# Summing the first layer's results inside the attention block, one group at a time

## The chip, the core and the metric

The kernel runs on one core of one Trainium2 chip. The metric is the device time of one launch in microseconds. The core has TensorE (PE in the profile; its weight loads are PEld), VectorE (DVE), ScalarE (ACT), GpSimd (POOL) and SyncE (SP), which here only issues transfers. Each engine runs its own instruction list in order, and the lists meet at semaphores.

## What is computed

Two layers over x, 32 sequences of 128 steps with 128 channels. In each layer a conditioning part feeds a mixture of experts, and the result is added to x.

```python
x = x + _L0_ffn_ref(_L0_cond_ref(cond_1024, x, ...), ...)       # layer 0: recurrence, then experts
x = x + _L1_ffn_ref(_L1_cond_ref(cond_1024, x, ...), ...)       # layer 1: attention, then experts

# layer 0: h = scan over 128 steps (gates z, r);  moe of 8 experts, top 2, plus 2 shared experts
w = jnp.sum(topk_probs[:, :, None] * onehot, axis=1)
return (shared + jnp.einsum('te,etd->td', w, y)).reshape(B, L, D)

# layer 1, attention
A = softmax(Q2 K2^T / sqrt(D)) - alpha * softmax(A1);  hidden = A @ V
# layer 1, experts: gates = top 2 of softmax(hidden @ wg), a capacity of C rows an expert
buf = zeros((E * C + 1, D)).at[pos].set(xk);  ...;  combined = sum(gates * ybuf[pos])
res = hidden + combined;  layer norm of res
```

## The kernel before

The program is three blocks one behind the other. In each block every engine has a list of its own, and between two blocks all engines meet at a barrier.

**Scan block** (`phase_scan`). The recurrence, layer 0's shared experts and its routed tiles. A tile's 256 result rows go to the DRAM tensor `moe_out` by two indirect transfers of 128 rows that GpSimd issues (`send`, L738 to L746); each row carries its own number, worked out once in `numbers` (L1272). `moe_out` has 2 x 4096 rows of 128 floats: half q holds each token's q-th expert. A row's number is sequence x 128 + step. At the end of the block the two halves are summed and turned, in eight groups of four sequences: SP loads group g of both halves into `yg[g % 3]` (L695), VectorE adds them (`add`, L1354), TensorE transposes four 128 x 128 pieces (`mix`, L916), and VectorE adds what the scan left in `xT` and writes `x1T` (`finish`, L1360). `x1T` is layer 1's input, channels on partitions. SP starts these loads when all results have landed (`y_sent`).

**Attention block** (`phase_attention`). Constants first (`constants`, `constants2`), then a software pipeline over the same eight groups, written out by hand in each engine's list. For group g: ScalarE makes the high part of `x1T` (`high`, L1662), VectorE the low part (`low`, L1722), TensorE queries and keys (`keys`, six matmuls of 512 columns, L351 to L353), values (`values`, 20 matmuls of 136 columns, L1566 to L1572), `scores` (L1588), the transposed weights (`turn_a`, L1579), router logits and hidden states (`attend`, L1598 and L1603), `x1T` turned to rows (`turn_x`, L1610) and the counts of tokens for each expert (`count`, L1619). VectorE picks the experts (`shifted`, `choices`, `gates`) and works out the slots (`places`, L1783 to L1795, which raises `pos_ready`). With `pos_ready` and the hidden states GpSimd issues 8 indirect transfers for the group, each sending 128 rows to their slots (`dispatch`, L327 to L335). Groups 0 to 6 are dispatched in this block, group 7 at the start of the next.

TensorE's order in iteration i is `keys(i+1)`, `values(i+1)`, `turn_a(i)`, `scores(i+1)`, `attend(i)`, `turn_x(i+1)`, `count(i)`. `turn_a` and `turn_x` write the one PSUM bank `bt`. ScalarE's `high(g)` waits for `values(g-1)`, since the tile `xg_hi` is one buffer.

**Expert block** (`phase_experts_norm`). It begins with the 8 transfers of group 7 (L2008); SP waits for all 64 (`sent_rows`, L1986) and loads the first expert's rows. Then come the eight experts, whose results go to `result_rows` by indirect transfers (L2017), and the tail: SP loads both halves group by group (L2001), the weighted rows are summed and normalised.

## Time and profile before

| | |
|---|---|
| median of 3 runs | 819.5 us (814.06 to 824.75) |
| profiled execution | 823.89 us, of which the span of instructions is 821.9 us |
| mean granted TensorE clock | 0.93 of full speed |
| PE, DVE, ACT, POOL busy | 85%, 67%, 58%, 49% of the span |
| scan block without the sums | 0 to about 475 us |
| sums of layer 0's results | about 475 to 497 us |
| attention block | about 497 to 601 us |
| barrier, group 7's dispatch, first load | about 601 to 622 us |
| experts | about 622 to 782 us |
| tail | about 782 to 822 us |

A row of the timeline reads: start in us from the span's start, duration, engine, line, operation, output and inputs, shapes, count; in brackets how long the engine had sat idle before it and what ended that. TensorE's matmuls overlap, so the time that one takes from its neighbours is the distance between starts.

### The profile page before, as it was taken

Reading aid. Unit: us, or ns where it says so; the run is one execution under the profiler, and the core shown is the slowest. Engines: PE = TensorE matmul, PEld = TensorE weight load, DVE = VectorE, ACT = ScalarE, POOL = GpSimd, SP = SyncE. Lnnn points to the kernel's source line nnn. Section 1 sums busy time; section 2 is a strip of 40 time slices with the busy share of each in tenths; the row PEclk is TensorE's granted clock in tenths of the full one; section 3 lists DMA queues with packets and bytes.
Section 4 is the critical chain, followed back from the end, with each engine's and each line's share of the span. In section 5 each row is a group of like instructions: output and inputs, shape, how many; then the busy total and the mean of one; then the engine's idle time right before and its main releaser. Section 6 shows DMA issues by size and latency. Waiting matters only on the chain. (4 is left out here: it accounts for less than half of the span.)

```text
span 821.9 us, 16651 instructions
## 1 busy us (share of the span) xinstructions
PE 696.3 (85%) x4698; PEld 610.9 (74%) x4698; DVE 550.4 (67%) x2312; ACT 473.8 (58%) x1393; POOL 402.6 (49%) x553
## 2 busy tenths in 40 slices
PE   5999999899999999998799737988617998999865
PEld 5988889898889888987799725877505877777621
DVE  2467677777877778776888654466635777677337
ACT  1355545565655666556799703354314887888446
POOL 0033334456667666656245600277750555656751
PEclk9999999999999999998999955799857999999978
DMA  8854522444433344434466271011114333310064
GB/s 231 223 132 125 131 70 75 141 138 138 145 110 116 107 143 144 138 136 148 160 221 219 82 204 53 12 51 52 52 42 126 88 112 97 115 38 19 21 179 128
DMA packets 98393, 95.77 MB, mean 117 GB/s; under 512 B 13793, under 2 KB 88870, under 8 KB 94206
## 3 DMA queue, kind: packets, MB, share of 16 engines
q1 hardware_dynamic: 83212, 75.36, 30.0%
q0 software_dynamic: 9216, 16.66, 6.4%
q10 hardware_dynamic: 5874, 2.68, 1.2%
q8 instruction: 38, 0.62, 0.3%
q14 instruction: 53, 0.43, 0.2%
HBM read 31.76 MB, written 31.61 MB: 77 GB/s over the span
## 5 line engine op out<-in xcount | busy, mean ns | idle before, releaser
L702 POOL CAST g_all<-g_f 128x256 fp32r<-128x256 f32 x196 | 88.5, 460 | 140.0 <-ACT g_f L1067 139.8
L1213 DVE TENSOR_TENSOR g_all<-g_f,g_all 128x256 fp32r<-128x256 f32 x288 | 120.3, 426 | 16.4 <-POOL g_all L702 9.4
L744 POOL DMA_INDIRECT moe_out<-wide,tag_to x80 | 80.9, 1011 | 56.2 <-DVE wide L1230 39.0
L2017 POOL DMA_INDIRECT result_rows<-yrow,dest x80 | 81.2, 1015 | 20.7 <-issue 19.5
L333 POOL DMA_INDIRECT slot_rows<-wide,posi x64 | 63.3, 989 | 49.4 <-DVE posi L1795 30.8
L351 PE MATMUL bank<-g_all,w_all 128*128 128x256 f32 (+1 forms) x256 | 82.4, 322 | 1.3 <-DVE g_all L2258 1.1
L1005 ACT ACTIVATE tr<-bank 128x32 f32<-128x32 f32 x128 | 25.3, 198 | 100.8 <-PE bank L794 99.0
L2154 ACT ACTIVATE g_f<-bank,b1c 128x512 f32<-128x512 f32 (+1 forms) x96 | 59.4, 618 | 39.2 <-PE bank L353 32.2
L1067 ACT ACTIVATE g_f<-bank,vecT 128x256 f32<-128x256 f32 x160 | 76.6, 479 | 5.4 <-DVE g_all L1213 3.6
L352 PE MATMUL bank<-g_all,w_all 128*128 128x256 f32 (+1 forms) x256 | 79.4, 310 | 0.0
L353 PE MATMUL bank<-g_all,w_all 128*128 128x256 f32 (+1 forms) x256 | 79.2, 309 | 0.0
L2258 DVE TENSOR_TENSOR g_all<-g_f,g_all 128x512 fp32r<-128x512 f32 (+1 forms) x96 | 55.9, 603 | 29.4 <-ACT g_all L2155 29.2
L734 POOL DMA_INDIRECT moe_rows<-raw,pos_all x64 | 63.8, 997 | 14.4 <-issue 13.5
L1157 DVE SCALAR_TENSOR_TENSOR zhh<-tz,hh 128x32 f32<-128x32 f32 x128 | 30.6, 239 | 51.7 <-ACT hh L1010 49.9
L1067 ACT ACTIVATE g_f<-bank,db 128x256 f32<-128x256 f32 x128 | 60.9, 476 | 6.7 <-PE bank L353 6.3
L794 PE MATMUL bank<-h,uh 128*128 128x32 f32 x256 | 49.0, 274 | 14.5 <-DVE h L1160 13.6
L1010 ACT ACTIVATE hh<-bank 128x32 f32<-128x32 f32 x128 | 25.6, 200 | 61.2 <-PE bank L802 60.3
L794 PEld LDWEIGHTS bank<-h,uh 128*128 128x128 f32 x256 | 39.5, 194 | 28.1 <-DVE h L1160 24.5
L2155 ACT ACTIVATE g_all<-bank,b1c 128x512 fp32r<-128x512 f32 (+1 forms) x96 | 59.0, 614 | 0.0
L351 PEld LDWEIGHTS bank<-g_all,w_all 128*128 128x128 f32 x256 | 48.6, 190 | 5.0 <-issue 2.3
L795 PE MATMUL bank<-h,uh 128*128 128x32 f32 x256 | 50.8, 281 | 0.0
L353 PEld LDWEIGHTS bank<-g_all,w_all 128*128 128x128 f32 x256 | 48.3, 189 | 2.9
(361 smaller groups left out, 2305.1 us busy)
## 6 DMA issues: line engine op xcount, KB each, us to landing
dw<-w_all SPq DMA_DIRECT2D x22, 1024.0 KB
g_all<-w_all SPq DMA_DIRECT2D x10, 1024.0 KB
wide<-moe_rows SPq DMA_DIRECT2D x40, 130.0 KB
slot_rows<-hs SPq DMA_DIRECT2D x8, 645.0 KB, 7.6
result_rows<-hs SPq DMA_DIRECT2D x8, 512.0 KB, 9.2
raw<-in_L_ffn_fc_w SPq DMA_DIRECT2D x16, 256.0 KB, 3.3
x1T<-result_rows SPq DMA_DIRECT2D x16, 256.0 KB, 3.4
x1T<-slot_rows SPq DMA_DIRECT2D x8, 387.0 KB, 4.3
```

The lines of the kernel that those rows point to most:

```text
L333: gp.indirect_dma_start(out=slots, out_offset=bass.IndirectOffsetOnAxis(ap=posi[:, i:i + 1], axis=0), in_=hid_rows[:, i // TOPK, :], in_of ...
L351: pe.matmul(out, a_hi, b_hi, start=start, stop=False, skip_group_check=True)
L352: pe.matmul(out, a_hi, b_lo, start=False, stop=False, skip_group_check=True)
L353: return pe.matmul(out, a_lo, b_hi, start=False, stop=stop, skip_group_check=True)
L702: gp.tensor_copy(ghi(u), gf(u)).then_inc(hi_ready, 1)
L734: gp.indirect_dma_start(out=moe_rows, out_offset=bass.IndirectOffsetOnAxis(ap=pos_all[:, i:i + 1], axis=0), in_=hrow[c % 2][:, o // TOPK, ...
L744: gp.indirect_dma_start(out=moe_out, out_offset=bass.IndirectOffsetOnAxis(ap=tag_to[:, i:i + 1], axis=0), in_=yrow[j % YR][:, k * P:(k + 1 ...
L794: pe.matmul(half(bank[0], 0)[:, ts], uh[:, P:2 * P], last, start=False, stop=False, skip_group_check=True).then_inc(r_acc, 1)
L1067: act.activation(gf(u), src, ACT.Gelu, bias=h1_bias(u), scale=0.5).then_inc(hidden_done, 1)
L1213: dve.tensor_tensor(glo(u), gf(u), ghi(u), ALU.subtract).then_inc(lo_done, 1)
L2017: gp.indirect_dma_start(out=results, out_offset=bass.IndirectOffsetOnAxis(ap=dest[q][:, j:j + 1], axis=0), in_=yrow[q][:, j * P:(j + 1) * ...
L2154: act.activation(g_f[u % 2][:, 0:w], hbank[u % 3][:, 0:w], ACT.Silu, bias=b_).then_inc(silu_done, 1)
```

## The change

- The sums leave the scan block. `add`, `mix` and `finish` and their loads now stand in the attention block, each some groups ahead of the group that needs them. `mix` writes the bank `bt`, so it takes turns with `turn_a` and `turn_x`.
- The order in each list changes. TensorE's iteration i is now `turn_a(i)`, `keys(i+1)`, `attend(i)`, `scores(i+1)`, `turn_x(i+1)`, `values(i+1)`, `count(i)`, `mix(i+3)`; for i = 0 `count` stands before `values`. `turn_a(i)` waits in addition for `finish(i+2)`. ScalarE's `high(i+2)` moves behind `weights(i+1)`. In VectorE's list `places(i)` moves behind `low(i+2)` (but for i = 0), and `finish(i+3)`, `add(i+4)` follow it.
- Row numbers in `moe_out` and `result_rows` become group x 512 + step x 4 + sequence within the group, so that a partition's four rows of a group lie together: the loads of both tensors read 2 KB runs instead of four runs of 512 bytes. `numbers` gets three more small VectorE operations and one more iota.
- GpSimd issues group 7's first four transfers at the end of the attention block and its last four in the next.
- SP loads expert 1's weights after `mix(6)` has read the buffer that they share; expert 0's before the fourth group's results.
- `x1rows` gets its own tile, `xg_hi` and `xg_lo` lie in `g_all`, and `nrm` and `fin` in `xT`.

The diff, cut to its core:

```diff
@@ phase_scan
-        y_src = moe_out.rearrange("(q g b p) c -> q g p b c", q=TOPK, b=GRP, p=P)
@@ SP
                 sp.wait_ge(zeroed, 16 * 2 * E)
-                for i in range(YR):
-                    sp.wait_ge(y_sent[i], 16 * CT * len(range(i, NJ, YR)))
-                for g in range(NG):
-                    ...
@@ PE
-                for g in range(NG):
-                    mix(g)
@@ DVE
                 def numbers():
...
+                    dve.tensor_tensor(fours[:], p_no[:].broadcast_to([P, P // GRP - 1]), fours[:], ALU.is_ge).then_inc(number_step, 1)
...
+                    dve.tensor_reduce(fourth[:], fours[:], AX.X, ALU.add).then_inc(number_step, 1)
...
-                for g in range(NG + 1):
-                    if g < NG:
-                        add(g)
-                    if g:
-                        finish(g - 1)
@@ phase_attention, SP
+                def results_in(g):
+                    if g >= YG:
+                        sp.wait_ge(mix_acc, g - YG + 1)
+                    for q in range(TOPK):
+                        sp.dma_start(yg[g % YG][q].rearrange("p (b c) -> p b c", c=P), y_src[q, g]).then_inc(yg_in[g % YG], 16)
+
+                for i in range(YR):
+                    sp.wait_ge(y_sent[i], 16 * CT * len(range(i, NJ, YR)))
+                for g in range(YG):
+                    results_in(g)
                 sp.wait_ge(w_conv, SPLIT)
-                for e in range(2):
-                    load_expert_weights(sp, d, raw, wts_in, e)
+                load_expert_weights(sp, d, raw, wts_in, 0)
+                for g in range(YG, NG):
+                    results_in(g)
+                sp.wait_ge(mix_acc, NG - 2 + 1)
+                load_expert_weights(sp, d, raw, wts_in, 1)
@@ POOL
                 for g in range(NG - 1):
-                    dispatch(gp, last_slot, g)
+                    dispatch(gp, last_slot, g, range(GRP * TOPK))
+                dispatch(gp, last_slot, NG - 1, range(LAST_HERE))
@@ PE
                 def turn_a(g):
                     pe.wait_ge(a_ready, (g + 1) * GRP)
                     pe.wait_ge(rows_done, g + 1)
+                    pe.wait_ge(mixed, min(g + 3, NG))
...
-                for i in range(-1, NG):
+                mix(0)
+                keys(0)
+                mix(1)
+                scores(0)
+                turn_x(0)
+                values(0)
+                mix(2)
+                for i in range(NG):
+                    turn_a(i)
                     if valid(i + 1):
                         keys(i + 1)
-                        values(i + 1)
-                    if valid(i):
-                        turn_a(i)
+                    attend(i)
                     if valid(i + 1):
                         scores(i + 1)
-                    if valid(i):
-                        attend(i)
+                        turn_x(i + 1)
+                    if i == 0:
+                        count(i)
                     if valid(i + 1):
-                        turn_x(i + 1)
-                    if valid(i):
+                        values(i + 1)
+                    if i:
                         count(i)
+                    if valid(i + 3):
+                        mix(i + 3)
@@ DVE
                 constants()
-                for i in range(-2, NG):
+                constants2()
+                add(0)
+                finish(0)
+                low(0)
+                add(1)
+                finish(1)
+                add(2)
+                for i in range(-1, NG):
+                    if valid(i):
+                        shifted(i)
+                        choices(i)
                     if valid(i + 1):
                         maxima(i + 1)
                     if valid(i):
-                        shifted(i)
+                        gates(i)
+                    if i == 0:
+                        places(i)
+                    if valid(i + 1):
+                        rows(i + 1)
+                        weights(i + 1)
                     if valid(i + 2):
                         low(i + 2)
...
+                    if i > 0:
                         places(i)
-                    if valid(i + 1):
-                        weights(i + 1)
-                        rows(i + 1)
+                    if valid(i + 3):
+                        finish(i + 3)
+                    if valid(i + 4):
+                        add(i + 4)
@@ phase_experts_norm
-                dispatch(gp, last_slot, NG - 1)
+                dispatch(gp, last_slot, NG - 1, range(LAST_HERE, GRP * TOPK))
```

How the lists stand in the compiled programs at three places. First TensorE in the attention block, between two iterations. Before: `turn_x`, `count` and the next iteration's `keys`.

```order
L1603 MATMUL bank<-v,amT 128x128 [waits hid_ready]
L1603 MATMUL bank<-v,amT 128x128 x3
L1610 MATMUL bank<-ident,x1T 128x128 [waits aT_ready]
L1610 MATMUL bank<-ident,x1T 128x128 x3
L1619 MATMUL bank<-masks_all,lowtri_b 128x64 [waits pos_ready,r_step]
L1622 MATMUL bank<-masks_all,ones_b 128x48
L1622 MATMUL bank<-masks_all,ones_b 128x32
L1622 MATMUL bank<-masks_all,ones_b 128x16
L1625 MATMUL bank<-masks_all,ones_b 128x16 x4
L351 MATMUL bank<-xg_hi,w_all 128x512 [waits q_ready,x_lo_ready]
```

Now the last matmul of `values`, then `count`, `mix` (L1645), `turn_a` (L1571) and `keys`.

```order
L1563 MATMUL bank<-cvr_lo,identr 128x136
L1613 MATMUL bank<-masks_all,lowtri_b 128x64 [waits pos_ready,r_step]
L1616 MATMUL bank<-masks_all,ones_b 128x48
L1616 MATMUL bank<-masks_all,ones_b 128x32
L1616 MATMUL bank<-masks_all,ones_b 128x16
L1619 MATMUL bank<-masks_all,ones_b 128x16 x4
L1645 MATMUL bank<-ident,raw 128x128 [waits rows_done,added]
L1645 MATMUL bank<-ident,raw 128x128 x3
L1571 MATMUL bank<-ident,am 128x128 [waits mixed,rows_done,a_ready]
L1571 MATMUL bank<-ident,am 128x128 x3
L353 MATMUL bank<-g_all,w_all 128x512 [waits q_ready,x_lo_ready]
```

`count` moved behind `values`, `mix` came in behind it, and `turn_a`, now first in the iteration, waits for `mixed`, which `finish` raises.

Second, VectorE in the same stretch. Before: the end of `places`, then `weights`, `rows`, `maxima`, `shifted` and `low`.

```order
L1793 TENSOR_SCALAR over<-rank_all 128x8
L1795 TENSOR_TENSOR posi<-pos,over 128x8 [waits r_step]
L1730 RECIPROCAL rinv<-rs 128x4 [waits p_ready]
L1736 TENSOR_SCALAR am<-pr,rinv,alphaT 128x128 [waits aT_acc,rinv_ready]
L1736 TENSOR_SCALAR am<-pr,rinv,alphaT 128x128 x3
L1740 TENSOR_TENSOR xT<-bank,beta_b 128x512 [waits rows_acc]
L1726 TENSOR_REDUCE nmax<-bank 128x4 [waits s_acc]
L1745 TENSOR_REDUCE lmax<-bank 128x4 [waits logit_acc]
L1747 TENSOR_TENSOR lsh<-bank,lmax 128x32 [waits r_step]
L1722 TENSOR_TENSOR xg_lo<-x1T,xg_hi 128x512 [waits x_hi_ready]
```

Now: the end of `weights`, `low` (L1740, whose output lies in `g_all`), the whole of `places`, `finish` (L1860) and `add` (L1855).

```order
L1754 TENSOR_SCALAR am<-pr,rinv,alphaT 128x128 x3
L1740 TENSOR_TENSOR g_all<-x1T,g_all 128x512 [waits x_hi_ready]
L1801 TENSOR_TENSOR loc<-bank,run 128x64 [waits rank_acc]
L1803 TENSOR_TENSOR sel<-loc,masks_all 128x64 [waits r_step]
L1804 TENSOR_TENSOR run<-run,bank 128x16
L1806 TENSOR_REDUCE rank_all<-sel 128x8 [waits r_step]
L1809 SCALAR_TENSOR_TENSOR pos<-rank_all,pos 128x4 [waits r_step]
L1809 SCALAR_TENSOR_TENSOR pos<-rank_all,pos 128x4
L1811 TENSOR_SCALAR over<-rank_all 128x8
L1813 TENSOR_TENSOR posi<-pos,over 128x8 [waits r_step]
L1860 TENSOR_TENSOR x1T<-xT,bank 128x512 [waits mix_acc]
L1855 TENSOR_TENSOR raw<-raw 128x512 [waits yg_in2]
```

`low`, `places` and `finish` now stand in one row, in that order, and `low` waits for ScalarE's `high`.

Third, SP at the seam of the first two blocks. Before, the loads of results stand ahead of the branch that ends the block; now they stand behind it.

```order
L661 DMA wg<-in_L_ffn_wg 128x8
L567 UNCONDITIONAL_BRANCH [waits zeroed]
L1501 UNCONDITIONAL_BRANCH [waits barrier_Pool_Activation_PE_DVE_SP_release]
L1507 DMA g_f<-moe_out 128x512 [waits y_sent2,y_sent1,y_sent0]
L1507 DMA g_f<-moe_out 128x512
L1507 DMA hs<-moe_out 128x512 x2
L1507 DMA raw<-moe_out 128x512 x2
L348 DMA raw<-in_L_ffn_fc_w 128x4x128 [waits att_w_ready]
L349 DMA raw<-in_L_ffn_fc_w 128x4x128
L1507 DMA g_f<-moe_out 128x512 [waits mix_acc]
```

The first load of results moved past the barrier, and a load is now one run of 512 floats a partition.

## Rows read from the trace of the kernel before

**Rows 1.** Chain that ended last: start, us, what; around the last dispatch
```profile
606.73 0.99 POOL slot_rows L333
...
615.70 2.45 DMA slot_rows<-wide,posi
```

**Rows 2.** Timeline: GpSimd's dispatches in the attention block, first and last
```profile
528.71 1.01 POOL L333 DMA_INDIRECT slot_rows<-wide,posi  x1 [29.86 <-DVE posi L1795]
...
599.97 0.97 POOL L333 DMA_INDIRECT slot_rows<-wide,posi  x1 [0.30 <-issue]
```

**Rows 3.** Block ends by line: duration ns min/median/max, first and last start us
```profile
L568 POOLq DRAIN  x1: 7947/7947/7947, 469.5 to 469.5; - x1
...
L1525 POOLq DRAIN  x1: 12554/12554/12554, 593.0 to 593.0; - x1
```

**Rows 4.** Timeline of the sums: first load, add, mix; last finish
```profile
474.74 0.93 SPq L695 DMA_DIRECT2D hs<-moe_out  x2
...
478.47 0.69 DVE L1354 TENSOR_TENSOR hs<-hs 128x512 f32<-128x512 f32 x1 [9.97 <-DMA hs<-moe_out]
...
479.22 1.11 PE L916 MATMUL bank<-ident,hs 128*128 128x128 f32 x4 [11.17 <-DVE hs L1354]
...
495.84 1.01 DVE L1360 TENSOR_TENSOR x1T<-xT,bank 128x512 f32<-128x512 f32 x1 [0.26 <-PE bank L916]
```

**Rows 5.** Timeline, VectorE and TensorE: front of the attention block
```profile
497.22 0.07 DVE L1799 MEMSET run<- 128x16 f32 x1 [0.36 <-PEq L568]
...
501.67 0.21 DVE L1829 TENSOR_SCALAR ones_b<-lowtri 128x128 bf16<-128x128 f32 x1
...
501.90 0.80 PE L351 MATMUL bank<-xg_hi,w_all 128*128 128x512 f32 x1
```

**Rows 6.** Timeline of TensorE: one iteration at full clock
```profile
546.07 0.48 PE L351 MATMUL bank<-xg_hi,w_all 128*128 128x512 f32 x1
...
547.55 0.23 PE L1566 MATMUL bank<-w_all,xg_hi 128*128 128x136 f32 x1
...
550.84 0.66 PE L1579 MATMUL bank<-ident,am 128*128 128x128 f32 x4
552.22 1.02 PE L1598 MATMUL bank<-v,amT 128*128 128x8 f32 x8
...
554.07 0.60 PE L1610 MATMUL bank<-ident,x1T 128*128 128x128 f32 x4
555.77 0.20 PE L1619 MATMUL bank<-masks_all,lowtri_b 128*128 128x64 bf16 x1 [1.11 <-DVE masks_all L1761]
```

**Rows 7.** Timeline: ScalarE's high, VectorE's low and places
```profile
550.94 0.63 ACT L1662 ACTIVATE xg_hi<-x1T 128x512 fp32r<-128x512 f32 x1 [2.51 <-PE bank L1572]
...
553.61 0.68 DVE L1722 TENSOR_TENSOR xg_lo<-x1T,xg_hi 128x512 fp32r<-128x512 f32 x1
...
556.42 0.22 DVE L1783 TENSOR_TENSOR loc<-bank,run 128x64 f32<-128x64 f32 x1
...
557.67 0.17 DVE L1730 RECIPROCAL rinv<-rs 128x4 f32<-128x4 f32 x1
```

**Rows 8.** Timeline of TensorE: the same work at half clock
```profile
511.29 0.79 PE L351 MATMUL bank<-xg_hi,w_all 128*128 128x512 f32 x1 [0.60 <-DVE xg_lo L1722]
...
514.02 0.32 PE L1566 MATMUL bank<-w_all,xg_hi 128*128 128x136 f32 x1
...
519.69 1.11 PE L1579 MATMUL bank<-ident,am 128*128 128x128 f32 x4
...
591.10 1.08 PE L1579 MATMUL bank<-ident,am 128*128 128x128 f32 x4 [3.55 <-DVE xT L1740]
```

**Rows 9.** Stretches: us, busy of PE, PEld, DVE, ACT, POOL; PEclk, DMA share, GB/s
```profile
523.00:570.00 47.00, 41.44 (x310) 36.09 (x310) 33.14 (x190) 25.06 (x78) 31.84 (x32) 1.00 0.14 45
570.00:574.00 4.00, 4.00 (x21) 3.80 (x21) 0.22 (x1) 1.23 (x2) 3.08 (x4) 0.57 0.19 54
...
591.00:594.00 3.00, 2.21 (x10) 1.84 (x10) 0.00 (x0) 0.60 (x1) 2.37 (x3) 0.50 0.20 65
```

More of the change, by code:

```diff
@@ L322, in build @@
         posi = sb("posi", [P, B * TOPK], U32)
+        y_sent = [sem(f"y_sent{i}") for i in range(YR)]
         hid_ready = sem("hid_ready"); pos_ready = sem("pos_ready"); sent_rows = sem("sent_rows")
@@ L325, in build, with dispatch @@
         hid_rows = wide[:].rearrange("p (b c) -> p b c", c=ROWW)
-        def dispatch(gp, last_slot, g):
+        def dispatch(gp, last_slot, g, parts):
             gp.wait_ge(hid_ready, g + 1)
             gp.wait_ge(pos_ready, g + 1)
-            for k in range(GRP * TOPK):
+            for k in parts:
                 i = g * GRP * TOPK + k
@@ L908, in count @@
                     t.then_inc(rank_acc, 1)
-                def mix(g):
-                    pe.wait_ge(added, g + 1)
-                    if g >= 2:
-                        pe.wait_ge(mixed, g - 1)
-                    for k in range(GRP):
-                        t = pe.transpose(bank[2 + g % 2][:, k * P:(k + 1) * P], yg[g % YG][0][:, k * P:(k + 1) * P], ident[:])
-                    t.then_inc(mix_acc, 1)
                 pe.wait_ge(ident_ready, 2)
@@ L1474, in phase_attention @@
         ones_b = sb("ones_b", [P, P], BF16)
-        xg_hi = sb("xg_hi", [P, GT], F32R)
-        xg_lo = sb("xg_lo", [P, GT], F32R)
+        xg_hi, xg_lo = (m["g_all"][:, i * GT:(i + 1) * GT] for i in range(2))
         qT = sb("qT", [P, GT])
@@ L1716, in _ @@
                         weights(i + 1)
+                    if valid(i + 2):
+                        high(i + 2)
+                    if valid(i + 1):
+                        values(i + 1)
             @block.vector
@@ L1739, in rows @@
                     dve.wait_ge(rows_acc, g + 1)
[L1740 removed]
+                    dve.tensor_tensor(v3(x1rows[:, g * GT:(g + 1) * GT], P), v3(bt[:], P), beta_b[:].unsqueeze(1).broadcast_to([P, GRP, P]), ALU.add).then_inc(rows_done, 1)
                 def shifted(g):
@@ L1873 @@
 RSTEPS = R_GATES + 7
+LAST_HERE = GRP
 SPLIT, WV_TURNED, CV_DONE, BQ_DONE, SETUP = 3, 3, 4, 5, 11
```

106 lines of the change are left out of this document (58 added, 48 removed).

## The prediction

> **What bounds the kernel now.** I read the busy times first: PE 85% says nothing alone, because the stages have different limits. Then the chain of waits. Ahead of the experts it runs through GpSimd's last transfers [rows 1], so what counts is when the transfer of group 7's last rows is issued. The first of its 8 issues starts at 606.73 and the last ends at 616.67 (its landing starts at 615.70; the seven before it 1.28 us apart). Every start in the expert block hangs on that end.
>
> Backwards from there: the timeline of GpSimd shows 56 issues from 528.71 to 599.97+0.97, with 0.30 us between two and nothing else [rows 2]. That is 71.26/55 = 1.296 us an issue on average; within a group 1.28. From the first to the last GpSimd never waits for a group, since TensorE's loop is about 9.9 us a group and 8 issues take 10.2. So in the attention block **GpSimd's issues are the bound**, and they begin 29.86 us late, when `posi` of group 0 is there. Then the drain at the block's end: it lasts till 593.0+12.55 = 605.55, 4.6 us past the end of the last issue [rows 3]; release, iota and a register bring the next issue to 606.73, 1.2 later.
>
> Ahead of it, the sums. SP's first load starts at 474.74, its add at 478.47, the last `finish` ends at 496.85 [rows 4]. Barrier and constants follow, and `keys(0)` starts at 501.90 [rows 5]. The scan's own end does not need the sums: GpSimd's drain there ends at 469.5+7.95 = 477.45 [rows 3].
>
> **The change, front.** The barrier now waits for that drain: release at about 477.7, where the sums ended at 496.85, so some 19.4 us earlier. The DVE constants take 501.88-497.22 = 4.7, nearly all that the first load needs as well (3.73 from its start to the add [rows 4]); say 482.1. Then, one behind the other, add 0.6, `mix` 1.1 (the clock is at half after the wait: its duration in [rows 4]), `finish` 1.03, `high` 0.63, `low` 0.68 [rows 4, 7]: `keys(0)` at 486.5, 15.4 earlier. What follows on TensorE is keys 2.7, `mix(1)` 1, scores 1.7, `turn_x` 1, values 3.3 (5.7 at half clock), and with `finish(1)` and `finish(2)` between: `turn_a(0)` at 498.5. Group 0's slots are ready about 9.7 later, as `attend`, the choice and `count` stand behind it: 508.2. **First dispatch at 509, 19.7 earlier.** If nothing else changed, that would all be won, as GpSimd is the bound.
>
> **The change, loop.** TensorE's pieces by distance between starts at full clock [rows 6]: keys 1.48, values 3.29, `turn_a` and scores 1.38, `attend` 1.85; `turn_x` is about 0.5. Sum 8.5; `count` and `mix` (0.2 and 0.5) are apart. Before, only 1.1 us of waiting on the masks lay in the pass [rows 6], and the period was 9.9.
>
> Now one row of work stands between `values(i+1)` and `turn_a(i+1)`: `high(i+2)` waits for `values(i+1)`, because `xg_hi` is one buffer; `low(i+2)` waits for `high`; VectorE has `places(i)` and `finish(i+3)` behind `low`; and `turn_a(i+1)` waits for `finish(i+3)`, since both use the bank `bt`. By [rows 4, 7]: 0.63 + 0.68 + 1.25 (556.42 to 557.67) + 1.03 = **3.6 us**. TensorE has 0.7 of its own to do there (`count`, `mix`). So it idles 2.9 us in each pass with a `finish`, that is i = 0 to 4, five passes: 8.5 + 3.6 = 12.1 to 12.2 us. (In pass 0 `places` is elsewhere, but `count` ahead of `values` waits instead.) That is more than GpSimd's 10.2: **TensorE and VectorE become the bound in five passes.** VectorE's wait for `high` costs `places` too, so group i's slots come about 1 us ahead of `turn_a(i+1)`.
>
> *The clock.* From 523 to 570 it was granted in full, with TensorE busy for 41.4 of 47 us and the gaps of 1.1 in it. It read 0.57 from 570 to 574, while TensorE was busy [rows 9]. Ahead of 591.10 TensorE had sat idle for 3.55 us [rows 8], and from 591 to 594 the clock was at 0.50, the lower level [rows 9]. A gap of 2.9 with 0.7 of small matmuls inside lies between the 1.1 that cost nothing and the 3.55 that did, nearer to the latter. I take a fall in each pass. Its price: keys 2.73 for 1.48 (511.29 to 514.02 [rows 8]), `turn_a` 1.11 for 0.66 long: 1.7 us, about as long as the fall at 570 to 574 lasted. Loop 12.2 + 1.7 = 13.9 us.
>
> The Trainium skill ("TensorE: Matmul & The Clock Gate", section "HAM oscillation — how this bites in real kernels") says that a loop whose idle stretch recurs loses the clock again in every pass and starts each burst cold. It is the rule that speaks against this change; without it (clock in full) the end would be that of rival A below. The rows at 591 agree for one gap; no row of before shows a recurring one.
>
> Walk: `turn_a(5)` at 498.5 + 5 x 13.9 = 568.0. The last passes have no `finish` and are held by VectorE's list, 10.2 each: `turn_a(6)` at 578.2, `turn_a(7)` at 588.4. Group 4's dispatch starts at 567.8 and is over at 578.0. Group 5's slots come 2.4 behind `turn_a(6)`, at 580.6, its first issue at 581.4. Groups 6 (590) and 7 (596.3) are ready in time. So 8 + 8 + 4 issues run one behind the other: 20 x 1.28 - 0.3 = 25.3, to 606.7. Drain 4.6, to 611.3; 1.2 to the first issue behind it, 612.5; the four left 4.8, to **617.3, against 616.67: +0.6**. The seam of the queue is dearer than it looks: before, 56 issues lay ahead of the drain and now 60.
>
> **Small terms.** `numbers` has three more dependent operations of VectorE in the scan's first chunk. The nearest row is a small one of 0.17 us [rows 7]: +0.5 if the scan waits there, 0 if not. The tail's first read comes in longer runs; a read of this size took 3.73 from its start to its use [rows 4]. No row separates runs from latency, so I bound it by 0 and a quarter of that, and take -0.5. Other loads of results were hidden behind one another before; now they come in during the loop, one group in 13.9 us, with 14% to 20% of the DMA engines busy there [rows 9]; nothing. `nrm`, `fin` and `x1rows` only change place. Expert 1's weights start at about `mix(6)`, near 555, some 60 us ahead of the experts: nothing; without that cover they would cost the few us of one load. ScalarE is 53% busy in the loop (25.06 of 47): no bound.
>
> Sum +0.6 + 0.5 - 0.5 = +0.6 on the profiled 823.9. That execution is 4.4 above the median of 819.5; I carry the difference to the median: 819.5 + 0.6 = **820 us**.
>
> **Rivals.**
> A, *the clock holds.* Gaps of 2.9 are too short to lose it. For: gaps of 1.1 did nothing, and the one that did was longer. Against: it fell once while TensorE was busy. Loop 12.2: five passes and the one behind them are 1.7 shorter each, and the front's `values` are partly at full clock (-2), so group 5's first issue is at 581.4 - 12.2 = 569.2, and the last of all ends at 617.3 - 12.2 = 605.1: -11.6, **808 us**.
>
> B, *`finish` is no wait.* If `high` is early (its wait covered by something I have not seen) the loop stays under 10.2 and GpSimd stays the bound: 509 + 60 x 1.28 = 585.8, + 4.6 + 1.2 + 4.8 = 596.4: -20, **799 us**. Against it: the four durations are rows, and the lists have no other place for them. It decides (16.4 us) from a loop under about 10.5: then group 5's first issue is at 564.4 and the end at 600.3.
>
> C, *the other side: the clock never comes back.* It is at half from 472 on at the front; before, `values` at 514 were still at the lower level, 12 us after `keys(0)` [rows 5, 8]. If each pass's gap keeps it down, the pieces are keys 2.73, values 5.67 (514.02 to 519.69 [rows 8]) and the rest likewise doubled: 15.6 + 3.6 = 19.3 a pass, 5 x 5.4 = +27, and the two last passes at 15.9 instead of 10.2, +11: +38, **858 us**. It decides (+16.4) from a loop of about 16.2, 2.3 more in each of seven passes. Against: a pass has over 8 us of unbroken matmuls, and `turn_a` to `attend` of the pass at 546 to 554 ran at full clock a few passes after the block's cold start [rows 6, 9].
> The Trainium skill (same page, "Part 4: PE-mode transpose") says that transposes do not count as busy for the clock in the way matmuls do, which speaks for C, since `mix`, `turn_a` and `turn_x` stand at the gap. No row of before tells transposes from matmuls here.
>
> D, *the change does not do what it says*: with GpSimd's drain at 477.45 not the last at the seam, the sums' 19.4 us would come back. SP has no load left there, and the three other engines only wait, so I give it no chance of its own; its time would be 820 + 19 = 839, on C's side.
>
> **Chances.** The forecast .70, A .17, B .07, C .06. The forecast's own range: loop between 12.9 and 14.4 (half of the clock's price, or values touched too), five times -1.0 to +0.5, and the small terms -1 to +1.2: 814 to 825. Over all: A's 808 with its bounds down to 805; above, a partial C (loop 14.9, +5) and the terms, 829. That leaves out B, C and little more. By 2%, about what a measurement of this kernel can tell from no change (803.1 and 835.9): faster .09 (B and the low end of A), slower .06 (C), same .85.
>
> **What would show it right or wrong** in the profile after: GpSimd's drain of the scan still ends near 477.5 and the barrier behind it; `keys(0)` near 486.5; first issue near 509; `turn_a` of groups 1 to 5 with about 2.9 us of idle ahead of it, ended by `x1T` of `finish`; period 13.9, with PEclk falling in every pass; gaps between groups in GpSimd's issues, and none behind group 5's first; last issue's end near 617. A period of 12.2 with full clock is A; no idle ahead of `turn_a` is B; PEclk 0.5 throughout is C. The forecast is wrong at its root if the first issue is not 15 us or more earlier, or if what is late between two groups is not `finish` but a load of results.

## The result, and the profile after

The changed kernel takes 825.17 us (median of 20 runs, 820.28 to 830.03), the kernel before 823.11 us beside it (median of 20 runs, 814.06 to 836.55). The ratio is 1.0049, interval 1.0029 to 1.0070: some half a per cent slower, less than the 2% that were to be told apart. Ratios, here and below, are of the undisturbed runs of both kernels and medians of all runs, so the two can differ where the runs spread. The profiled execution takes 826.30 us, its span 824.6 where 821.9 stood before.

| | before | forecast | after |
|---|---|---|---|
| scan's last result issued | 472.56 | the same, +0.5 at most | 476.29 |
| DVE starts the constants | 497.22 | about 477.7 | 481.50 |
| `keys(0)` | 501.90 | 486.5 | 490.33 |
| `turn_a(0)` | 519.69 | 498.5 | 501.85 |
| first dispatch | 528.71 | 509 | 511.93 |
| period in the loop (`turn_a` to `turn_a`) | 9.9 | 13.9 | 12.9 in the first pass, then 13.7 to 14.0 |
| last dispatch ends | 616.67 | 617.3 | 619.64 |
| from there to the end of the span | 205.2 | 204.7 | 205.0 |

First the timeline of GpSimd after the change, the rows that answer to [rows 2, 3]. The number in brackets is the idle time ahead of a row and what ended it.

```profile
476.29 0.97 POOL L737 DMA_INDIRECT moe_out<-wide,tag_to  x1 [0.30 <-issue]
482.17 0.20 POOL L1523 MEMSET lowtri<- 128x128 f32 x1 [4.90 <-POOLq L567]
...
511.93 0.99 POOL L334 DMA_INDIRECT slot_rows<-wide,posi  x1 [28.73 <-DVE posi L1813]
...
528.48 0.97 POOL L334 DMA_INDIRECT slot_rows<-wide,posi  x1 [6.06 <-DVE posi L1813]
...
542.31 0.97 POOL L334 DMA_INDIRECT slot_rows<-wide,posi  x1 [3.93 <-DVE posi L1813]
...
556.06 0.97 POOL L334 DMA_INDIRECT slot_rows<-wide,posi  x1 [3.85 <-DVE posi L1813]
...
569.77 0.97 POOL L334 DMA_INDIRECT slot_rows<-wide,posi  x1 [3.79 <-DVE posi L1813]
...
583.44 0.97 POOL L334 DMA_INDIRECT slot_rows<-wide,posi  x1 [3.78 <-DVE posi L1813]
...
607.74 0.97 POOL L334 DMA_INDIRECT slot_rows<-wide,posi  x1 [0.30 <-issue]
614.07 0.15 POOL L2048 IOTA slot_no<- 128x10 f32 x1 [5.36 <-POOLq L1500]
...
618.67 0.97 POOL L334 DMA_INDIRECT slot_rows<-wide,posi  x1 [0.30 <-issue]
```

Where [rows 2] had 0.30 throughout, GpSimd now waits for `posi` ahead of each of groups 1 to 5: 6.06, 3.93, 3.85, 3.79 and 3.78 us. These five waits are 21.4 us, 19.9 more than five times 0.30. That is where the gain of the early start (16.8 us) went, all of it and 3 us more.

What is late there is told by the timelines of ScalarE, VectorE and TensorE in one pass (`high`, `low`, first of `places`, `posi`, `finish`, `turn_a`, first of `keys`).

```profile
538.97 0.63 ACT L1679 ACTIVATE g_all<-x1T 128x512 fp32r<-128x512 f32 x1 [1.21 <-PE bank L1563]
539.63 0.69 DVE L1740 TENSOR_TENSOR g_all<-x1T,g_all 128x512 fp32r<-128x512 f32 x1 [0.52 <-ACT g_all L1679]
540.24 0.22 DVE L1801 TENSOR_TENSOR loc<-bank,run 128x64 f32<-128x64 f32 x1
541.36 0.17 DVE L1813 TENSOR_TENSOR posi<-pos,over 128x8 uint32<-128x8 f32 x1
541.44 1.00 DVE L1860 TENSOR_TENSOR x1T<-xT,bank 128x512 f32<-128x512 f32 x1
542.59 1.09 PE L1571 MATMUL bank<-ident,am 128*128 128x128 f32 x4 [2.83 <-DVE x1T L1860]
543.33 0.78 PE L353 MATMUL bank<-g_all,w_all 128*128 128x512 f32 x1
```

From `high` at 538.97 to `turn_a` at 542.59 it is 3.6 us of one row behind another, and TensorE is idle for 2.83 of them. The `turn_a` of group 1 waited 1.47 us for `finish`, those of groups 2 to 5 waited 2.93, 2.83, 2.74 and 2.69. Three stretches of about one pass each, columns as in [rows 9]:

```profile
525.50:539.40 13.90, 10.97 (x73) 9.59 (x71) 8.31 (x40) 5.57 (x17) 7.77 (x8) 0.75 0.23 77
539.40:553.20 13.80, 10.97 (x73) 9.49 (x71) 8.34 (x40) 5.55 (x17) 7.77 (x8) 0.75 0.13 41
553.20:567.00 13.80, 11.06 (x72) 9.48 (x71) 8.33 (x40) 5.61 (x18) 7.78 (x8) 0.75 0.25 76
```

TensorE is busy for 11.0 us of each 13.8, and the granted clock is 0.75 in each, that is half of the time at 1.2 GHz and half at 2.4 GHz.

Where in the pass the clock falls is told by shorter stretches around one wait. TensorE's last row ahead of it, `mix`, ends at 553.61, and `turn_a` starts at 556.35.

```profile
549.60:553.00 3.40, 3.40 (x29) 2.84 (x28) 3.00 (x13) 1.78 (x9) 2.01 (x3) 1.00 0.19 60
553.10:553.60 0.50, 0.50 (x3) 0.11 (x1) 0.21 (x1) 0.50 (x3) 0.00 (x0) 0.50 0.00 0
553.65:556.30 2.65, 0.00 (x0) 0.00 (x0) 2.55 (x11) 0.28 (x1) 0.24 (x1) 0.50 0.51 152
```

The clock is already at its lower level for the last half microsecond of TensorE's work: by the records it falls at 553.08, ahead of the idle stretch and not in it, after 10.5 us in which TensorE was never idle. In all five passes it falls ahead of the idle stretch: at 512.12, 525.77, 539.43, 553.08 and 566.73, where TensorE's work ends at 513.28, 525.83, 539.77, 553.61 and 567.36. At 525.77 the two all but coincide. The fall of 553.08 is over at 559.91, 6.8 us later. At 580.39 the clock falls once more, again after 10 us of unbroken work, and there the `turn_a` (580.35) had waited for nothing.

### The profile page after: what moved, and what is told of

The parts are those of the page before. It is cut to its first block and busy times, and to the rows that moved or that the text cites. A ratio compares the mean times of both kernels' runs of the same rounds, so it can differ in the third digit from the quotient of the medians.

```text
span 824.6 us, 16658 instructions
## 1 busy us (share of the span) xinstructions
PE 702.3 (85%) x4698; PEld 617.4 (75%) x4698; DVE 549.3 (67%) x2315; ACT 474.7 (58%) x1393; POOL 401.9 (49%) x554
## 5 line engine op out<-in xcount | busy, mean ns | idle before, releaser
L353 PE MATMUL bank<-g_all,w_all 128*128 128x256 f32 (+1 forms) x272 | 93.7, 345 | 3.9 <-DVE g_all L1740 2.5
L2058 POOL DMA_INDIRECT result_rows<-yrow,dest x80 | 81.1, 1014 | 20.7 <-issue 20.4
L354 PE MATMUL bank<-g_all,w_all 128*128 128x256 f32 (+1 forms) x272 | 89.5, 329 | 0.0
L355 PE MATMUL bank<-g_all,w_all 128*128 128x256 f32 (+1 forms) x272 | 89.1, 328 | 0.0
L787 PE MATMUL bank<-h,uh 128*128 128x32 f32 x256 | 49.5, 276 | 14.8 <-DVE h L1142 13.8
L353 PEld LDWEIGHTS bank<-g_all,w_all 128*128 128x128 f32 x272 | 54.0, 199 | 9.2 <-DVE g_all L1740 3.3
L355 PEld LDWEIGHTS bank<-g_all,w_all 128*128 128x128 f32 x272 | 53.8, 198 | 4.4
L354 PEld LDWEIGHTS bank<-g_all,w_all 128*128 128x128 f32 x272 | 53.9, 198 | 3.4
```

Source lines behind the costliest of these rows:

```text
L353: pe.matmul(out, a_hi, b_hi, start=start, stop=False, skip_group_check=True)
L354: pe.matmul(out, a_hi, b_lo, start=False, stop=False, skip_group_check=True)
L355: return pe.matmul(out, a_lo, b_hi, start=False, stop=stop, skip_group_check=True)
L787: pe.matmul(half(bank[0], 0)[:, ts], uh[:, P:2 * P], last, start=False, stop=False, skip_group_check=True).then_inc(r_acc, 1)
L2058: gp.indirect_dma_start(out=results, out_offset=bass.IndirectOffsetOnAxis(ap=dest[q][:, j:j + 1], axis=0), in_=yrow[q][:, j * P:(j + 1) * ...
```

## Experiments

Four sets ran, each on a chip of its own, and all kernels of a set on one chip beside the kernel before. The chips fell into two kinds: on the one of the third set the kernel before takes 825 us, as in the result; on those of the first, second and fourth it takes 880, 867 and 870. So ratios are compared within a set, and periods with the set they are from.

**First set: parts of the wait, one by one, and the clock alone** (kernel before 880.25).

`e1_finish_first`, in VectorE's list:

```diff
-                    if i > 0:
-                        places(i)
                     if valid(i + 3):
                         finish(i + 3)
+                    if i > 0:
+                        places(i)
```

> VectorE's finish(i+3) ahead of places(i) instead of behind it, nothing else. My theory (turn_a waits for finish, and finish stands behind high, low and places): the idle ahead of turn_a shrinks from 2.9 to about 1.6 us, the period from 13.8 to about 12.5 if the clock still falls in each pass, places come 1.0 later. Five passes win 1.25 each, places lose 1: about -5 against the changed kernel, near 820. If the gap of 2.9 is what makes the clock fall and 1.6 is short enough, 1.7 more in each pass: period about 10.9, -13, near 812. Rival (GpSimd is what sets the end again whatever the period): no change, 825.

`e2_two_buffers` (`keys`, `values` and `low` take `xg[g % 2]` too):

```diff
-        xg_hi, xg_lo = (m["g_all"][:, i * GT:(i + 1) * GT] for i in range(2))
+        xg = [[m["g_all"][:, (2 * k + i) * GT:(2 * k + i + 1) * GT] for i in range(2)] for k in range(2)]
...
-                    if g:
-                        act.wait_ge(v_acc, 2 * g)
+                    if g > 1:
+                        act.wait_ge(v_acc, 2 * (g - 1))
```

> Two buffers for the high and the low part, so that high(i+2) need not wait for values(i+1); the lists are unchanged. My theory: what is left behind values is count, places 1.25 and finish 1.0, so turn_a idles 1.8 instead of 2.9 and the period is about 12.7 with the clock falling, 11.0 without: -5 (near 820) or -13 (near 812). Rival (high and low are not in the way, only places and finish are): the idle ahead of turn_a stays 2.9, 825.

`e3_mix_inside`, in `values` of TensorE (the call behind `count` is gone) and in VectorE's list:

```diff
                         t.then_inc(v_acc, 1)
+                        if k == 0 and g and g + 2 < NG:
+                            mix(g + 2)
...
+                    if valid(i + 3):
+                        finish(i + 3)
                     if valid(i + 2):
                         low(i + 2)
                     if i > 0:
                         places(i)
-                    if valid(i + 3):
-                        finish(i + 3)
```

> mix(i+3) between the two halves of values(i+1), and finish(i+3) ahead of low(i+2) and places(i) in VectorE's list; one buffer as before. My theory: nothing but 0.6 us is left ahead of turn_a, the period falls to about 10.1, the clock stays at full, GpSimd's 10.2 us a group is the bound again and no gap is left between its groups. First dispatch as in the changed kernel at about 512, last one ends at 512 + 64 x 1.28 + 6 = 600 instead of 619.6: -19, near 806. Rival (the clock falls in each pass even with TensorE busy, since transposes don't hold it): period about 11.7, -10, near 815.

`e5_fill`:

```diff
                     if valid(i + 3):
                         mix(i + 3)
+                        pe.wait_ge(hid_ready, i + 1)
+                        for k in range(11):
+                            pe.matmul(bh[:], w_hi[:, 0:P], w_hi[:, 0:512], start=True, stop=True, skip_group_check=True)
```

> The stall stays, but TensorE fills it in five passes with 11 matmuls of 512 columns into a free bank, whose results nobody reads (2.4 to 2.8 us at full clock). It prices the clock alone. My theory (the gap makes the clock fall): clock at full throughout the loop, period 12.2 instead of 13.8, -8, near 817. Rival (the clock falls for another reason): clock still falls in each pass, the fill then costs 4.7 us where it meets the lower clock, period 14 to 16, 825 to 835.

| | median | ratio to the kernel before (interval) | last dispatch starts |
|---|---|---|---|
| e1_finish_first | 878.21 | 0.998 (0.993 to 1.003) | 660.81 |
| e2_two_buffers | 879.25 | 1.003 (0.998 to 1.009) | 664.17 |
| e3_mix_inside | 878.58 | 0.997 (0.992 to 1.002) | 657.72 |
| e5_fill | 876.88 | 0.999 (0.994 to 1.004) | 660.77 |

No ratio is clear of 1, and the changed kernel was not among them. The profiles say more, with that of the changed kernel from the next set beside them, on another chip of this kind; there it has a period of 17.5, in an execution of 880.90 us where its median is 872.19, so this control is a long one. With `finish` first `turn_a` waited for it 2.0 us on average (8.0 us in four passes) against 3.2 (12.9 in four) and the period is 15.9 to 16.9. That is the 1.2 less that `places` takes. With two buffers alone the period is 17.6 and the wait 3.3 us (13.1 in four): nothing won. There VectorE came to `low` behind its own work, so `high` was not what it waited for; my theory for this one was wrong on this chip. The passes of `e3_mix_inside` take 14.4 to 17.1 us where theory and rival had 10.1 and 11.7, and those of `e5_fill` 13.6 to 17.0 where they had 12.2 and 14 to 16; the clock is at 0.61 to 0.91 and at 0.76 to 0.87 in stretches of 14 us. Every pass is longer on this chip, and neither run decides there.

**Second set: the changed kernel again, and the layout alone** (kernel before 867.15). `f0_changed_again` is the changed kernel, `f3_mix_inside` and `f5_fill` are the edits above. `f6_layout_alone` is the kernel before with the change's `numbers`, row patterns and nothing else:

```diff
-        y_src = moe_out.rearrange("(q g b p) c -> q g p b c", q=TOPK, b=GRP, p=P)
+        y_src = moe_out.rearrange("(q g p b) c -> q g p b c", q=TOPK, b=GRP, p=P)
```

> The changed kernel itself, as the control of this set. In the first set every kernel, the one before too, took about 880 us instead of 823, and in the traces engines that wait for TensorE start up to 4.4 us after the recorded end of the matmul. If that belongs to the chip and not to my edits, the changed kernel shows it here too or not at all, together with the others. Expected: ratio to the kernel before 1.005 as measured first.

> The kernel with mix between the halves of values and finish ahead of low and places, again, beside its control. My theory: period near 10.1, no gaps between GpSimd's groups, last dispatch some 19 us earlier than in the changed kernel, near 600: ratio to the kernel before about 0.98. Rival (the clock falls in each pass even without the gap): period about 11.7, ratio about 0.993. The first set, where all periods were 14 to 18, left this open.

> The stall filled with 11 matmuls that nobody reads, again, beside its control. My theory (the gap makes the clock fall): clock at full in the loop, period 12.2 instead of 13.8, 8 us under the control. Rival: the clock falls all the same, period 14 to 16, at or above the control.

> The kernel before with the new row numbers alone: the three more operations in numbers, the runs of 2 KB for the loads of both result tensors; the sums stay in the scan block. My theory: the sums' loads come faster than one group in 2.2 to 2.8 us, so VectorE (0.7 + 1.0 a group) is the bound there and the sums end about 5 us earlier; numbers costs nothing to 0.5; the tail's first read -0.5: -5, ratio 0.994. Rival one (numbers is what made the scan 3.7 us longer in the changed kernel's profile): the scan's last result is issued near 476 instead of 472.6, and the kernel is at 0 to -2. Rival two (the loads are bound by latency, not by the length of the runs): sums as before, ratio 1.000.

| | median | ratio to the kernel before (interval) |
|---|---|---|
| f0_changed_again | 872.19 | 1.011 (1.006 to 1.016) |
| f3_mix_inside | 865.26 | 0.994 (0.989 to 1.000) |
| f5_fill | 866.57 | 1.000 (0.996 to 1.003) |
| f6_layout_alone | 869.49 | 0.992 (0.986 to 0.998) |

Against the changed kernel on the same chip, the wait taken away wins 1.6% by the ratios and 0.8% by the medians, the fill 1.1% and 0.6%. The fill leaves the wait in and adds work, so what it wins (9 us by the ratios, 5.6 by the medians; 8 were expected) is part of the price of the clock; in its profile the clock is at 0.76 to 0.88 in the loop and not at full. The runs of f6_layout_alone spread from 855.70 to 878.70, and its median (above that of the kernel before) and its ratio (below 1) point different ways: its time does not tell what the layout is worth.

The control shows the late releases of the first set too, so they go with the chip and not with one of the edits. The rows are of TensorE (`scores`, `turn_x`) and VectorE (`maxima`) in the changed kernel on this chip:

```profile
585.26 1.92 PE L1580 MATMUL bank<-kT,qT 128*128 128x128 f32 x8
586.96 0.71 PE L1604 MATMUL bank<-ident,x1T 128*128 128x128 f32 x4
...
589.38 0.69 DVE L1744 TENSOR_REDUCE nmax<-bank 128x4 f32<-128x512 f32 x1 [3.55 <-remote]
```

`scores` is recorded as ended at 587.18 and its reader starts 2.2 us later, with VectorE idle. In the result's chip the same reader came 0.3 us behind. No run tells what is slow there.

The layout alone seems to have shortened the sums; this is one execution against one, on different chips. In VectorE's timeline (first add, first `finish`, last `finish`):

```profile
497.42 0.69 DVE L1363 TENSOR_TENSOR hs<-hs 128x512 f32<-128x512 f32 x1 [9.61 <-DMA hs<-moe_out]
...
500.10 1.03 DVE L1369 TENSOR_TENSOR x1T<-xT,bank 128x512 f32<-128x512 f32 x1
...
512.37 1.01 DVE L1369 TENSOR_TENSOR x1T<-xT,bank 128x512 f32<-128x512 f32 x1 [0.26 <-PE bank L919]
```

From 497.42 to 513.38 it is 16.0 us, where [rows 4] have 18.4: 2.4 won, half of the 5 expected, as loads still end three of VectorE's waits behind the first.

**Third set, on a chip like the result's** (kernel before 824.88). `g3_mix_inside` and `g5_fill` as above; `g4_both` has `e2_two_buffers` and `e3_mix_inside` together.

> mix between the halves of values, finish ahead of low and places, a third time. On the two chips so far (the kernel before takes 867 and 880 us there) the clock stays low for most of each pass and the period is 15 to 17. If this is a chip like the first (before at 823): period near 10.1, no gap between GpSimd's groups, ratio to the kernel before about 0.98. If it is a chip like the last two: ratio near 0.994 as there.

> The same and two buffers for the high and low parts, so that high does not wait for values either. On a chip like the first, GpSimd's 10.2 us a group are the bound in both, so my theory says the same time as with one buffer, ratio 0.98. If TensorE's pass is the bound still (as on the slower chips), this one is some 0.6 to 1 us a pass shorter than with one buffer, -3 to -5.

> The stall filled with 11 matmuls that nobody reads, a third time; on the last chip it took 9.4 us off the changed kernel. On a chip like the first my theory says clock at full in the loop and a period of 12.2 instead of 13.8, last dispatch near 611, ratio to the kernel before 0.995. If the clock falls for another reason than the gap: period 14 or more.

| | median | ratio to the kernel before (interval) | last dispatch starts |
|---|---|---|---|
| changed kernel (the result) | 825.17 | 1.005 (1.003 to 1.007) | 618.67 |
| g3_mix_inside | 825.18 | 0.999 (0.995 to 1.004) | 618.51 |
| g4_both | 813.88 | 0.991 (0.987 to 0.996) | 612.84 |
| g5_fill | 819.73 | 0.997 (0.993 to 1.001) | 611.89 |

The fill did what it was to do. GpSimd's timeline shows three periods of 12.13 and one of 13.05, where 12.2 was expected, and the stretches show the clock at full in two of three:

```profile
527.26 0.96 POOL L334 DMA_INDIRECT slot_rows<-wide,posi  x1 [6.07 <-DVE posi L1816]
...
539.39 0.97 POOL L334 DMA_INDIRECT slot_rows<-wide,posi  x1 [2.23 <-DVE posi L1816]
...
551.52 0.97 POOL L334 DMA_INDIRECT slot_rows<-wide,posi  x1 [2.23 <-DVE posi L1816]
...
564.57 0.97 POOL L334 DMA_INDIRECT slot_rows<-wide,posi  x1 [3.12 <-DVE posi L1816]
```

```profile
525.50:539.40 13.90, 13.31 (x89) 11.04 (x87) 10.12 (x48) 5.50 (x16) 7.78 (x9) 1.00 0.23 76
539.40:553.20 13.80, 13.46 (x86) 11.74 (x86) 9.14 (x42) 5.51 (x16) 9.14 (x10) 0.88 0.28 83
553.20:567.00 13.80, 13.35 (x92) 11.43 (x90) 7.89 (x39) 6.81 (x19) 8.36 (x9) 1.00 0.13 40
```

So with the gap filled, the clock stays at full for most of the loop; its one fall, at 548.67, lasts 3.4 us. The Trainium skill ("TensorE: Matmul & The Clock Gate", section "HAM oscillation — how this bites in real kernels") says that a loop with an idle stretch in it pays for the clock in every pass; the changed kernel's three passes at 0.75 and this kernel's at 1.00, 0.88 and 1.00 agree. That section of the Trainium skill has the clock fall in the idle stretch; in the changed kernel it fell 0.1 to 1.2 us ahead of it.

With the wait taken away it went otherwise than I expected. TensorE's timeline of g3_mix_inside, `turn_a` of two passes and rows behind the second (`keys`, then the logits):

```profile
530.68 0.63 PE L1573 MATMUL bank<-ident,am 128*128 128x128 f32 x4
...
541.19 0.63 PE L1573 MATMUL bank<-ident,am 128*128 128x128 f32 x4
542.35 0.50 PE L353 MATMUL bank<-g_all,w_all 128*128 128x512 f32 x1 [0.53 <-DVE g_all L1740]
...
543.27 0.63 PE L353 MATMUL bank<-g_all,w_all 128*128 128x512 f32 x1
...
544.55 1.71 PE L1592 MATMUL bank<-v,amT 128*128 128x8 f32 x8
```

A pass at full clock takes 10.5 us (530.68 to 541.19) with no wait for `finish`, as the theory has it. But at 543.0 the clock falls, to come back at 549.8, and that pass takes 13.4 us. Since 516 TensorE had stood still for no more than 0.6 us at a time. Its stretches:

```profile
512.00:526.00 14.00, 12.84 (x50) 11.39 (x51) 5.90 (x25) 3.90 (x8) 8.21 (x8) 0.51 0.27 75
526.00:540.00 14.00, 12.58 (x94) 10.89 (x92) 11.53 (x53) 6.91 (x24) 4.86 (x5) 1.00 0.19 58
...
568.00:582.00 14.00, 13.79 (x70) 12.02 (x68) 6.92 (x38) 5.64 (x17) 8.70 (x9) 0.62 0.14 44
```

A pass at full clock is followed by one or two in which it is low for much of the time. The whole loop, from `turn_a(0)` to `turn_a(7)`, in the changed kernel and then in this one:

```profile
501.85:590.95 89.10, 76.23 (x483) 65.62 (x483) 53.42 (x268) 38.01 (x111) 45.33 (x46) 0.77 0.18 55
```

```profile
501.19:591.27 90.08, 84.15 (x483) 74.19 (x483) 55.02 (x268) 37.31 (x111) 47.09 (x48) 0.75 0.19 58
```

TensorE is idle for 5.9 us instead of 12.9 and busy for 7.9 more with the same 483 matmuls. In the changed kernel 12.8 of the 41.3 us of low clock lay in its idle time; here nearly all of 44.9 lies in its work. So the last dispatch is only 0.2 us earlier than in the changed kernel: **the 7 us of idle that were removed came back as work at half clock**. That was the rival of this run. With two buffers as well, the clock is low for 38.0 us of a loop of 83.2 and the last dispatch is 5.8 us earlier; 813.88 us is the best time of the study, 0.9% under the kernel before by the ratio.

**Fourth set: why the clock falls without a gap** (kernel before 869.68, a chip of the slower kind). `h_both_fill` is g4_both and

```diff
+                        if k == 0 and g:
+                            pe.wait_ge(hid_ready, g)
+                            fill(3)
                         if k == 0 and g and g + 2 < NG:
                             mix(g + 2)
...
                         count(i)
+                    if valid(i + 1):
+                        pe.wait_ge(hid_ready, i + 1)
+                        fill(3)
```

> Two buffers, mix between the halves of values, and in each pass 3 matmuls that nobody reads ahead of mix and 3 behind count. The set before showed full-clock passes of 10.4 to 10.5 us without the wait, but they were followed by passes at half clock though TensorE stood still for no more than 0.6 us at a time, while the fill of the long gap kept the clock up. My theory now (what holds the clock is how much of the time is real matmuls; waits, and transposes too, count against it): with 1.4 us more of them a pass the clock stays up, the pass takes 11 us, the last dispatch starts near 605 instead of 611.8, ratio to the kernel before about 0.985 against 0.991 without the fill, on a chip like the first. Rival (the falls are due to heat or supply, and more matmuls only bring more of them): half-clock passes stay as many and each pass is 1.4 to 2.8 us longer, ratio 1.00 or above.

Measured: 863.83 us, ratio 0.996 (0.992 to 1.000), clock 0.98 in the first full stretch of the loop and 0.63 to 0.87 in those behind it, periods of 14 to 18. It does not decide between the two theories: on this kind of chip all periods are long, and TensorE had gaps of up to 4.5 us again (ahead of 578.9). Why the clock falls in g3_mix_inside and g4_both, where no gap is longer than 0.6 and 0.8 us behind the loop's first pass, stays open.

## Why the prediction came out

The forecast was 820 us, its own range 814 to 825; 825.17 is 0.2 above it, and inside the 805 to 829 of the whole. Of the 5.2 us between, 3.6 are the base: 819.5 was the median of three runs of the kernel before, and 20 runs have 823.11. The change itself was forecast at +0.6 and came at +2.1.

**Where the bound is: right.** Before, GpSimd never waited in the loop; after, it waits in each pass that has a `finish`, for `posi`, and no longer behind group 5's first issue. The end of the last dispatch moved by +3.0 and the span by +2.7.

**The front: right in size, on a later base, and in one place by luck.** From the constants' start (481.50) to `keys(0)` it is 8.8 us, forecast 8.8. `turn_a(0)` is 20.4 behind the constants, forecast 20.8; the first dispatch 30.4, forecast 31.3. Inside, two errors cancel: the 498.5 counts `values(0)` at half clock, 5.7 us, and it took 3.4 at full; and `turn_a(0)` waited 1.93 us for `finish`, for which the sum has no term. What moved all of them is the scan.

**The small term of the scan: the one mis-sized.** I allowed +0.5 for `numbers`, and -1 to +1.2 for all small terms together. The scan's last result was issued 3.7 us later than in [rows 4]'s execution (476.29 against 472.56). It is lost in three jumps, as the start of one operation that VectorE makes in every step of the scan (`zhh`) shows, steps counted from 0:

| step | before | after | later by |
|---|---|---|---|
| 2, just ahead of `numbers` | 23.27 | 23.50 | 0.2 |
| 4, behind `numbers` | 31.23 | 31.45 | 0.2 |
| 5 | 33.56 | 34.94 | 1.4 |
| 48 | 146.52 | 147.76 | 1.2 |
| 54 | 162.23 | 165.01 | 2.8 |
| 108 | 320.65 | 322.97 | 2.3 |
| 114 | 339.04 | 343.53 | 4.5 |

`numbers` itself costs nothing: the distance is the same ahead of it and behind it. Its price was 0 and not 0.5, and the term that was missing is the clock in the scan. The first jump is seen in the same seven matmuls, before and after:

```profile
31.09 1.07 PE L821 MATMUL bank<-identr 128*128 128x256 f32 x7
```

```profile
31.32 1.84 PE L814 MATMUL bank<-identr 128*128 128x256 f32 x7
```

They take nearly twice as long, as at half clock, though PEclk reads 1.00 from 22 to 37 us in both kernels. Six of the twelve profiled executions of the changed scan have this long step (3.4 to 3.6 us from step 4 to 5), the other six and f6_layout_alone have 2.2 to 2.3 as the kernel before. The other two jumps are falls of the clock. The stretches 145 to 160 and 335 to 350, first before, then after:

```profile
145.00:160.00 15.00, 13.19 (x104) 12.05 (x103) 10.81 (x58) 8.50 (x33) 5.59 (x10) 1.00 0.51 174
335.00:350.00 15.00, 14.22 (x117) 13.32 (x117) 12.37 (x63) 10.52 (x41) 8.70 (x14) 1.00 0.49 172
```

```profile
145.00:160.00 15.00, 13.94 (x90) 12.89 (x90) 9.35 (x50) 6.90 (x28) 3.71 (x9) 0.79 0.47 165
335.00:350.00 15.00, 13.49 (x101) 12.95 (x101) 10.62 (x50) 8.13 (x32) 6.66 (x14) 0.89 0.46 164
```

The three kernels of the third set have the same scan as the changed kernel; they issue the last result at 476.3, 475.7 and 474.7. The fall at 335 to 350 (0.89) is in all three, the one at 145 to 160 in one. Four of the eight profiles of the same scan on the slower chips (e1_finish_first, e2_two_buffers, f3_mix_inside, h_both_fill) have 1.00 all the way from 320 to 375. So the scan ended 2 to 4 us later in four executions of the changed scan than in the one execution of before, and all three jumps are absent in some executions of the same code; why the clock is lower in them is open. More than one profile of before would have shown how far the scan's end moves by itself.

**The loop: right in the wait and in the sizes, not in the reason for the clock.** The wait is the one named, in its own size in four of five passes: 2.93, 2.83, 2.74 and 2.69 us of idle against 2.9 (1.47 in the first). The period is 13.7 to 14.0 in these four against 13.9. The clock's price of 1.7 us a pass is confirmed by the fill: 12.13 against 13.8.

The fall in each pass was taken from the length of the gap: 2.9 us lies nearer to the 3.55 that cost the clock than to the 1.1 that did not. The fall came in each pass, but ahead of the gap, by 0.1 to 1.2 us; at 580.39 and in g3_mix_inside the clock fell without one. So the length of the gap is not shown to be the reason, and that the forecast of a fall in each pass came true is in part luck. What the fill shows is less: with matmuls in the gap the clock stays up over most of the loop. The comparison of 1.7 us with the time that the fall at 570 to 574 lasted is a misreading too: that one lasted 3.4 us (570.40 to 573.82), which costs 1.7 where TensorE works all the while.

**The end: 2 us late.** Group 5's first issue was forecast at 581.4 and came at 583.44, 2.0 late. The seam took what was forecast: from the last issue's end at 608.71 to the first behind the barrier at 614.83 it is 6.1 us, forecast 5.8.

**The tail's first read: right in sign.** In the chain of waits of after it landed in 2.89 us:

```profile
785.43 2.89 DMA x1T<-result_rows
```

Before it took 3.50, so 0.6 less against the 0.5 taken. From the last dispatch's end to the end of the span 0.3 were won.

**The sum.** From the constants' start to the last dispatch's end the changed kernel takes 138.1 us, forecast 139.6: 1.5 too much in the walk, against 3.2 too little for the scan. The forecast of +0.6 and the measured +2.7 (span) or +2.1 (medians) differ by these two, and 0.2 less were won in the tail; part of the good agreement is that the two have opposite signs.

**The rivals.** A, full clock in the loop, is what the fill made: its period is A's 12.2, its last dispatch ends at 612.9 and not at A's 605.1. Of the difference, the first issue at 510.65 instead of 509 is 1.7; the rest is in the first pass, 16.6 between the first issues of groups 0 and 1, and in the one of 13.05, whose stretch has the one fall of the clock. B, no wait at all, was built (g3_mix_inside) and did not give its 799: the wait went, the clock fell all the same. I had priced B with the clock at full, as if a pass without a gap were enough for that. C did not come on this kind of chip; on the slower kind the changed kernel's clock is 0.66 to 0.67 in stretches of 20 us of the loop and its period 17.5, longer than C's bound of 16.2, but the kernel with the old order has a longer period there too (13.5), so no verdict of C's follows.

## What to carry to other kernels

When one bound hides another, a start that is 17 to 20 us earlier is worth nothing unless the loop behind it keeps pace: work out the period of every engine in the new order before the gain is booked. What one engine writes last in a pass should not stand behind three rows of another engine's list if the next pass opens with it; here the transposes could go into the middle of `values`. And a wait taken away from TensorE is priced only when the clock of the stretch without it is known: here, on the chip like the result's, it gave back nothing by itself, while filling the wait with matmuls that nobody reads won 0.8 to 1.1% against the changed kernel by the ratios (7 to 9 us; 5.4 and 5.6 by the medians). The smaller figure compares with the result's set, not with a changed kernel of its own; and against the kernel before, the fill's ratio of 0.997 (0.993 to 1.001) is not clear of 1. Only both edits together are (g4_both, 0.991).

## What the runs showed of the hardware

- In the changed kernel the clock fell in each of five passes 0.1 to 1.2 us before TensorE's idle stretch of 1.5 to 2.9 us began (553.08 against 553.61), and at 580.39 after 10 us without an idle stretch.
- The granted clock fell to half with TensorE never idle for more than 0.6 us (g3_mix_inside at 543.0). It stayed full over most of the passes whose gap was filled with matmuls (g5_fill: 1.00, 0.88, 1.00). TensorE is recorded as busy for 12.6 to 13.8 of 14 us in g3_mix_inside and for 13.3 to 13.5 of 13.8 in g5_fill.
- The kernel before took 823 and 825 us in the result and in the third set, and 867 to 880 us on three other chips. On the latter, engines that read TensorE's banks start up to 5.5 us after the recorded end of the matmul (2.2 in the rows above; 5.5 in f5_fill at 588.87, where `maxima` had stood idle for 5.0), and the periods in the attention's loop are mostly 2 to 4 us longer, that of the kernel with the old order too (13.5 in f6_layout_alone against 9.9). The chip was not varied alone, so what differs between them is not known.
- Falls of the clock in the scan, to 0.79 and 0.89 in stretches of 15 us, made the scan 1.5 and 2.2 us later and come and go between executions of the same code.
- At 31 us seven matmuls of 256 columns took 1.84 us in one execution and 1.07 in another, with PEclk at 1.00 in both: the profile's clock seems not to show every stretch at half clock.
